# A decoder kernel on Trainium2: GpSimd's weight splits in smaller pieces and in other places

## What is computed

```python
x = x + _L0_attn_ref(_layernorm(x), W_q, W_kv, W_o)      # 1: attention in Fourier space, 16 heads
x = x + _L0_xattn_ref(_layernorm(x), k, bias, ctx, ctx, 8) # 2: long convolution with the context
x = x + _L0_ffn_ref(_layernorm(x), W1, b1, W2, b2, W3, b3, Wg, bg)  # 3: 8 experts, top 2
x = x + _L1_attn_ref(...)    # 4: latent attention with rotary positions
x = x + _L1_xattn_ref(...)   # 5: int8 fake-quantised cross attention
x = x + _L1_ffn_ref(...)     # 6: ternary weights, gated
```

```python
gate_weights = softmax(x @ Wg + bg)
topv, topi = top_k(gate_weights, 2)
h = gelu(x @ W1[n] + b1[n]); h = gelu(h @ W2[n] + b2[n]); eo = h @ W3[n] + b3[n]
out = sum over the two chosen experts of topv * eo
```

## Time and profile before

| | us |
|---|---|
| median of 3 runs | 723.18 |
| lowest and highest run | 721.86, 723.79 |
| the profiled execution | 724.21 |
| its span | 722.4 |

### The profile page before, as it was taken

One profiled execution on the slowest core, in us unless ns is written; L12 is line 12 of the kernel. 1 busy time (PEld: TensorE's weight loads), 2 busy tenths in 40 slices (PEclk: granted clock), 3 DMA queues, 4 the chain that ended last, 5 costly groups with the idle time before them and its releaser, 6 DMA issues.

```text
span 722.4 us, 12069 instructions
## 1 busy us (share of the span) xinstructions
PE 558.2 (77%) x4141; PEld 394.7 (55%) x4143; DVE 430.5 (60%) x994; ACT 300.2 (42%) x742; POOL 253.3 (35%) x297
## 2 busy tenths in 40 slices
PE   3949699258369999999979989979888367763665
PEld 2538344156248888887635656656575155643233
DVE  3586899946545555554572544535465647767773
ACT  1421200242534444443423745727573455545553
POOL 3950478854700000000576954908622200010000
PEclk9969999655679999999988999999999789885886
DMA  8592410444751111110220000000000500000000
GB/s 293 171 371 95 145 59 0 150 157 149 243 189 53 46 46 45 46 44 24 81 88 1 1 0 1 1 0 1 1 1 1 175 2 2 2 2 0 8 22 30
DMA packets 32248, 49.62 MB, mean 69 GB/s; under 512 B 3096, under 2 KB 22368, under 8 KB 31808
## 3 DMA queue, kind: packets, MB, share of 16 engines
q1 hardware_dynamic: 29888, 41.65, 17.4%
q0 software_dynamic: 2304, 7.21, 2.8%
HBM read 39.68 MB, written 9.18 MB: 68 GB/s over the span
## 4 chain that ended last, share of the span: by engine, by line
PE 58%; DVE 18%; ACT 12%; POOL 4%; issue 4%; DMA 3%; SPq 0%; ACTq 0%; DVEq 0%; POOLq 0%
PE bank L1565 14%; PE bank L1580 4%; PE bank L1735 4%; PE bank L1675 3%; POOL sorted_rows L499 3%; PE bank L1697 3%; PE bank L1671 2%; PE bank L1724 2%; PE bank L1443 2%; PE bank L1708 2%; ACT sm L722 2%; ACT pT L824 2%; DVE xn L930 2%; PE bank L1980 2%; PE bank L1472 1%
## 5 line engine op out<-in xcount | busy, mean ns | idle before, releaser
L667 ACT ACTIVATE hf<-bank,be 128x256 f32<-128x256 f32 (+1 forms) x120 | 44.3, 420 | 67.4 <-PE bank L1565 53.4
L505 POOL DMA_INDIRECT yg<-expert_rows,pos x16 | 15.8, 988 | 156.0 <-DMA expert_rows<-yb 151.5
L1565 PE MATMUL bank<-h,wsp 128*128 128x256 f16 (+1 forms) x720 | 67.6, 249 | 1.7 <-DVE h L1123 1.6
L1565 PEld LDWEIGHTS bank<-h,wsp 128*128 x720 | 57.2, 97 | 11.1 <-issue 4.8
L1121 DVE CAST h<-hf 128x512 f16<-128x512 f32 (+1 forms) x60 | 21.8, 364 | 56.6 <-ACT hf L667 55.2
L487 POOL TENSOR_TENSOR kvp<-xnT,cxT 128x512 f32<-128x512 f32 x32 | 35.7, 1139 | 42.8 <-issue 33.3
L577 ACT CAST wsp<-wraw 128x2048 f16<-128x2048 f32 x12 | 22.7, 1900 | 66.6 <-DMA wraw<-in_L_ffn_W 66.6
L722 ACT ACTIVATE sm<-sm,nm 128x128 f32<-128x128 f32 x128 | 49.9, 395 | 0.6 <-DVE nm L1236 0.6
L465 POOL TENSOR_TENSOR wsp<-wraw,wsp 128x512 f16<-128x512 f32 x40 | 45.8, 1178 | 9.1 <-ACT wsp L577 8.8
L1233 DVE SCALAR_TENSOR_TENSOR sm<-bank,const 128x512 f32<-128x512 f32 x32 | 22.1, 691 | 38.9 <-PE bank L1697 38.9
L524 POOL TENSOR_TENSOR sm<-sm,rinv 128x512 f32<-128x512 f32 x32 | 33.1, 1040 | 24.9 <-DVE rinv L1227 24.9
(11 more groups left out here) (299 smaller groups left out, 1337.3 us busy)
## 6 DMA issues: line engine op xcount, KB each, us to landing
wraw<-in_L_ffn_W SPq DMA_DIRECT2D x16, 512.0 KB, 5.2
wraw<-in_L_ffn_W SPq DMA_DIRECT2D x8, 1024.0 KB, 7.0
cxT<-in_ctxT SPq DMA_DIRECT2D x2, 1024.0 KB, 7.6
tap<-in_taps SPq DMA_DIRECT2D x1, 2048.0 KB, 14.1
xg<-sorted_rows SPq DMA_DIRECT2D x8, 256.0 KB, 2.8
expert_rows<-yb SPq DMA_DIRECT2D x8, 256.0 KB, 2.2
sorted_rows<-early POOLq DMA_DIRECT2D x1, 1536.0 KB, 13.1
sorted_rows<-early POOLq DMA_DIRECT2D x1, 1408.0 KB, 16.3
```

The source lines that it names most:

```text
L667: last = nc.scalar.activation(hf[:, p, n * k:n * k + n], bank[2 * (layer - 1) + p][:, n * k:n * k + n], ACT.Gelu, bias=be[:, layer - 1, u, ...
L1565: last = nc.tensor.matmul(b[:, n * (f % 2):n * (f % 2) + n], w[a_][:, c, P * f:P * f + P], inp[:, b_, c, :], start=(c == 0 and a_ + b_ == ...
```

## The change

POOL's casts and subtractions go from 4 pieces of 512 columns to 16 pieces of 128 for every half it handles. On ACT, `split_high(4)` and `(5)` move into the loop of `kqT` copies of sublayer 1, ahead of tile 2; `(6)` and `(7)` stand behind the wait for the zero fill; `(8)` moves ahead of the `xnT` copies of the third norm. On POOL, `split_low(4)` and `(5)` move ahead of the `kvp` products; `(6)` and `(7)` follow them; `(8)` and `(9)` wait for the whole third norm (`xn_ready`). On SP, the loads of expert 3 move ahead of the wait for the end of sublayer 1.

```diff
@@ shape constants @@
-QUARTERS = 4
+PIECES = 16
@@ SP @@
                 for half in range(2):
-                    if e >= 2:
+                    if e == 2 or e >= 4:
                         expert_half(e, half)
                 if e == 2:
+                    expert_half(3, 0)
+                    expert_half(3, 1)
                     x_done(sp, 1, NT - 1)
@@ POOL @@
+            def pieces(k):
+                return [(2048 // PIECES * q, 2048 // PIECES) for q in range(PIECES)]
+
             def split_low(k):
...
-                for q in range(QUARTERS):
-                    part = slice(cols.start + 512 * q, cols.start + 512 * q + 512)
-                    last = nc.gpsimd.tensor_tensor(wsp[:, e, 1, part], wraw[:, half, 512 * q:512 * q + 512], wsp[:, e, 0, part], ALU.subtract)
+                for at, n in pieces(k):
+                    part = slice(cols.start + at, cols.start + at + n)
+                    last = nc.gpsimd.tensor_tensor(wsp[:, e, 1, part], wraw[:, half, at:at + n], wsp[:, e, 0, part], ALU.subtract)
...
-                for q in range(QUARTERS):
-                    part = slice(2048 * (k % 2) + 512 * q, 2048 * (k % 2) + 512 * q + 512)
-                    last = nc.gpsimd.tensor_copy(wsp[:, k // 2, 0, part], wraw[:, k % 2, 512 * q:512 * q + 512])
+                for at, n in pieces(k):
+                    part = slice(2048 * (k % 2) + at, 2048 * (k % 2) + at + n)
+                    last = nc.gpsimd.tensor_copy(wsp[:, k // 2, 0, part], wraw[:, k % 2, at:at + n])
...
                 pool.dma_start(xs[P * lo:P * hi, :].rearrange("(b p) d -> p b d", p=P), zeros[:, 0:hi - lo]).then_inc(sem("zero_filled"), 16)
+            split_low(4)
+            split_low(5)
             pool.wait_ge(sem("xnT_act"), 4)
...
-            for k in range(POOL_HALVES, 10):
-                split_low(k)
+            split_low(6)
+            split_low(7)
+            pool.wait_ge(sem("xn_ready"), 3 * NT)
+            split_low(8)
+            split_low(9)
@@ ACT @@
             for t in range(NT):
+                if t == 2:
+                    split_high(4)
+                    split_high(5)
                 act.wait_ge(sem("kq_psum"), t + 1)
...
             xnT_copies(2)
-            for k in range(POOL_HALVES, 6):
-                split_high(k)
             act.wait_ge(sem("zero_filled"), 32)
             split_high(6)
+            split_high(7)
...
             deviation(3)
-            split_high(7)
+            split_high(8)
             xnT_copies(3)
-            split_high(8)
             split_high(9)
```

## The result

| | before | after |
|---|---|---|
| median, us | 723.5 | 737.8 |
| lowest and highest run | 721.9, 725.2 | 734.7, 739.6 |
| the profiled execution (its span) | 724.2 (722.4) | 739.6 (737.8) |

Four runs of each; the ratio is 1.0188, 95% interval 1.0158 to 1.0218: slower by 14.3 us.

A forecast was written before the change was run, and what follows sets the result against it. It saw a sequence of stages with no engine busy throughout. Stage 1 at +19.5 us less stage 3's 3.9 gave +15.6, so 739.8 for the profiled execution and 739 for the median; range 726 to 748.

The forecast's parts named there:

- The piece: On POOL, a 128-column subtraction takes 0.49 us and a cast 0.25, so a half takes 11.9 instead of 6.8.
- smaller constant: Rival on POOL: plain tiles have a smaller constant, pitch 0.42 us, a half takes 10.0, total 731; chance 0.17.
- The fourth split: On POOL in stage 1, it ends and its load is issued at 64.6 instead of 43.7.
- columns alone: Rival: POOL pieces cost 0.28 us, halves stay at 6.8; net -10, 713 us, or 720 with another +5; chance 0.13.
- The load, the cast, the restart of PE: Stage 1: load lands after 6.1 us, ACT's cast takes 1.9, PE's slow restart adds 2.0.
- just fit in: With old POOL times, ACT's moved splits would fit in its 10.54 us of idleness before copy 2 at 55.10.
- stage 1: Copy 2 of kqT on ACT starts 17.5 us late, PE restarts +2.0; the stage ends 19.5 later.
- each meeting of DVE and POOL at one piece: A DVE operation beside POOL's splits waits for about one POOL instruction, through an exclusive lock on a shared port.
- Stage 3: Third norm, gate and routing: gain of 5.4 less a loss of 1.5 gives 3.9 us, ends 1.5 and 7.4.
- norm and gate: Third norm: small operations gain 2.1 us, first four xn 3.0, the rest 0.3; gate matmuls 5.4 earlier.
- What arrives: Stage 3's 3.9 us gain reaches the experts in full; first expert matmul near 221 instead of 205.4.
- the rival with the right piece: Rival on POOL: with a smaller constant for plain tiles a half takes 10.0 us, total 731; chance 0.17.

The follow-up runs named there:

- e1: The changed kernel with POOL's pieces back at 512 columns, its new order kept; 727.5 us, ratio 1.0055 to the kernel before.
- e4: The changed kernel, with POOL waiting for its own semaphore after every fourth piece and each half's end from k = 4 on; 732.8 us, ratio 1.0130 to before.
- e8: The changed kernel with split_high(4) and (5) moved behind ACT's loop of kqT copies; 718.4 us, ratio 0.9933 to the kernel before.
- v1: The kernel before with 128-column pieces, POOL's waits after every fourth piece for k = 4 to 9, and ACT reordered around the third norm; 718.4 us, ratio 0.9913.
- v2: The changed kernel with split_high(4) and (5) behind ACT's kqT loop and POOL waiting after every fourth piece from k = 4; 715.2 us, ratio 0.9903 to before.
- e3: The changed kernel with 512-column pieces for k = 0 to 3 and 128 for k = 4 to 9; 726.2 us, ratio 1.0064 to before.
- e5: The changed kernel with one wait of POOL on its own piece, after piece 8 of k = 4 and of k = 8; 735.4 us, one run.
- e6: The changed kernel with one wait of POOL on its own piece, after piece 4 of k = 4 and of k = 8; 737.8 us, one run.
- e7: The changed kernel with 64-column pieces for k = 4 and up; 738.3 us, one run.
- e2: The kernel before with POOL's pieces at 128 columns and nothing else; 724.7 us, ratio 1.0029 to before.

## Why the prediction was right, and which of its steps were not

The total was right: 739 forecast, 737.8 measured, and the first expert matmul at 220.78, where I had put it near 221. In each of the two stages, steps were wrong by sizes that cancelled.

**The piece.** I took 0.49 for a subtraction, from the L517 row, and 11.9 for a half; 0.385 and 10.1 were measured. The casts were right (0.25, measured 0.24). The rival "smaller constant" had the half at 10.0. What failed is the choice between rows: the product of 128 columns with the inner step of two was the wrong neighbour. Before's 512 pieces (1.12) and after's 128 (0.385) give 0.14 us that doesn't shrink and 1.9 ns a column: a constant, as I had argued, but half of the 0.3 that I read out of unlike instructions. The estimate of 0.32 from the Trainium skill (GPSIMD Engine Reference, Instruction dispatch and the cycle accounting behind it) was nearer to 0.385 than my 0.49. The fourth split ended at 59.36 instead of 64.6. The pieces would have brought it 7 earlier; but POOL lost 4.1 us to DVE between 14.99 and 59.36 (44.4 us for four halves of 10.1), 3 more than before, where I had allowed 0.5. One slip of a rival: "columns alone" with another 5 us comes to 718 by its own terms (713 + 5), not 720.

**The load, the cast, the restart of PE.** 6.1, 1.9 and +2.0 were forecast; 6.1 (59.39 to 65.49), 1.9 and 3.67 for a group instead of 1.73 were measured. e1 shows that the 6.1 depends on the moment: issued at 43.97 the same load took 14.6. That my figure fitted was luck. The trace of before held this price already, for the very load that SP issues at 43.70 (us from issue to landing, view of its line):

```profile
DMA to landing us min/median/max: 15.9/15.9/15.9
```

It landed at 59.6, after the 55.10 of copy 2: with the old POOL times the splits would not have "just fit in", and "columns alone" could not have left stage 1 as it was. I had overlooked it, and taken the figure from other loads. Copy 2 came 12.2 late, not 17.5.

**What I left out.** One product then stood 6.3 us behind POOL's run, so that PE's group came 17.3 later than the 57.44 of before and ended 19.1 later; stage 1 was to be 19.5 longer, and `kvp` indeed starts at 98.79 instead of 79.28. I had priced each meeting of DVE and POOL at one piece. The rows that I rested this on the earlier trace rows are 512-column pieces, and there it holds. The Trainium skill (SBUF — State Buffer, Who interferes with whom) says that a DVE instruction with two inputs in SBUF contends with a GpSimd instruction that reads SBUF, and that issue order decides who blocks. The waits of about one piece in e1, e4 and e8 agree. 6.34 and 6.72 us beside pieces of 0.385 go beyond it: 15 and 17 more instructions of POOL started ahead of a waiting DVE.

**Stage 3.** Forecast: norm and gate +5.4, routing -1.5, together 3.9. Measured: gate matmuls at 163.64 instead of 150.48, 13.2 later where stage 1 had put 19.5 on, a gain of 6.3 (POOL's run was over at 156.30, before the first `nw`, where I had it reach into the norm); another 3.0 from the clock in the matmuls; and the routing from `lg` to `pos` took 18.1 instead of 12.6 (157.48 to 170.10), a loss of 5.5. Together 3.8. The sum was right, each part was not. e4 confirms that the held operation carries the loss: without it `lg` to its successor takes 0.25.

**What arrives.** The scatter starts at 186.78 instead of 171.10 (+15.7) and the experts 15.4 later, as forecast: nothing else was late next.

Had the holds not come, my error on the piece would have shown: e4, without them, took 732.8, near the 731 of the rival with the right piece, and by an estimate it would have taken some 3 less with gate matmuls of 4.0 us instead of 7.0. The prediction was right in its mechanism, that ACT's queue in the loop waits for POOL's fourth split, which e8 shows by undoing it alone. It was right in its number partly by chance.

## What to carry to other kernels

Before a step is moved into an engine's in-order loop, add up the whole chain that its input waits for (here POOL's split, a load, a cast), and put it behind the loop if that chain has less slack than the change takes from it; behind the loop ACT's casts cost nothing here. Smaller pieces on POOL shorten what DVE waits as long as DVE comes early in a run or takes turn after turn (the second norm in e8); against the long holds POOL has to stop now and then: a wait on its own semaphore every fourth piece cost 0.03 us a piece and took away holds of 6 us. Price a small instruction from two sizes of the same instruction, not from its neighbours in the table.

## What the runs showed of the hardware

- A DVE operation with both inputs in SBUF stood up to 6.7 us behind 128-column subtractions of POOL that ran back to back, if it came 5.7 us or more after POOL's last stop or DVE's last turn (seven operations), and took under 0.8 if it came within 4.6. Beside 128-column casts it stood 2.1 and 2.4 us after 4.0 and 3.9 us (v1, v2). What decides it is open.
- An operation with one input was held too: the third norm's `ve`, 11.9 us into a run, took 0.44 to 0.48 instead of 0.17 in six kernels, each until the run ended. DVE's additions from PSUM and its statistics beside the same run (0.67 to 0.75 for the ones from 149.71 on in the changed kernel) took what they take without POOL.
- POOL's subtraction starts every 1.12 us with 512 columns, 0.385 with 128 and 0.27 with 64.
- A load of 1 MB took 6.1 us when issued at 59.39 and 14.6 when issued at 43.97, in the same order of work (e1); in the kernel before, issued at 43.70, it took 15.9.
- The same 32 gate matmuls ran at a granted clock of 0.50 in the kernel before, e1, e3, e4, e5, e6, e8 and v1 (7.0 us each), and at 0.91 in the changed kernel (4.0), 0.89 in e7 (4.1), 0.78 in e2 (4.6) and 0.71 in v2 (5.0). What PE did in the microseconds ahead was alike (16 transposes in 3.4 to 3.8 us), so what decides it is open; up to 3 us of such a stage are not to be credited to an edit.
